# Routing and table writing moved earlier, and the two early-started attentions rearranged, in a twelve-block kernel on one core

## The chip, the cores and the metric

The kernel runs on one core of one Trainium2 chip. The metric is the device time of one execution in microseconds (us). "Before" is the kernel as it stands, "after" the changed one. TensorE does matrix products, VectorE and ScalarE elementwise work, GpSimd elementwise work and the indirect (row by row) transfers, SyncE only issues transfers.

## What is computed

Four layers work in turn on `x` of 4 x 512 x 128 (batch, position, feature), each with a feed-forward part, an attention or recurrence, and the feed-forward part once more. Cut to what matters:

```python
x = x + 0.5 * L0_ffn(layernorm(x))     # moe0_0: 8 experts, best 1, capacity 320
x = x + L0_attn(layernorm(x))          # att0: 16 heads, relative bias, causal
x = x + 0.5 * L0_ffn(layernorm(x))     # moe0_1
x = x + 0.5 * L1_ffn(layernorm(x))     # ffn1_0 (best 2 of 8 gated experts, dense)
x = x + L1_attn(layernorm(x))          # att1
x = x + 0.5 * L1_ffn(layernorm(x))     # ffn1_1
x = x + 0.5 * L2_ffn(layernorm(x))     # ffn2_0 (best 2 of 8 linear experts, dense)
x = x + L2_rec(layernorm(x))           # rec2
x = x + 0.5 * L2_ffn(layernorm(x))     # ffn2_1
x = x + 0.5 * L3_ffn(layernorm(x))     # moe3_0: 8 experts, best 2, capacity 512
x = x + L3_attn(layernorm(x))          # att3: a layernorm, gamma and beta of its own inside, all positions seen
x = x + 0.5 * L3_ffn(layernorm(x))     # moe3_1
```

In a mixture (`moe...`) each token goes to the expert with the highest gate logit (layer 3: to the best two), takes the next free slot of it, in token order, and is dropped when the slots are full. Layer 3 gives slots to all first choices ahead of all second ones.

## The kernel before

`x` stays on the chip as 16 tiles of 128 tokens; a batch `b` (0 to 3) is four tiles. One block of code follows another. A block has a program for each engine, run in order, with semaphores between them, and all engines meet at its end. At some ends the semaphores used so far are cleared as well.

**Routing** (`Routing`). For a batch, `choose` (VectorE) finds the expert from the gate logits, `count` (TensorE) counts earlier tokens of the same expert, `place` (VectorE) makes slot numbers, and `scatter` (GpSimd, L573) issues one indirect transfer for each tile into `dispatched`, a table in HBM. For layer 3 there are `choose(1)`, `count_second`, `place_second` and a second scatter of `second_rows`. The table is first filled with a row that marks a slot as unused (`write_untaken`, L229); no scatter may start before that has landed.

**Mixture** (`moe_capacity`). The load of the first slots waits for all scatters. Eight experts follow (L726, L733). Results go back by indirect transfers (L923) to `returned`, come back as `moe_back`, and VectorE adds them to `x` by batch: `add_rows` (L890), then statistics (`stats`), the power of -1/2 on GpSimd (L108, or L143 for the double norm of layer 3), then the normalised rows (L117 or L150). TensorE transposes these (L172) and ScalarE copies the columns (L184, L181).

**The first block** (`Lead`, in moe0_0) also loads `x` and routes all batches itself. **The start of an attention** (`AttentionStart`, `begun` or `follow`) lies in the mixture ahead of att0 and att3: queries and keys of batch 0 are projected (L1714), taken (L1721) and split into three bf16 parts. High and middle parts are casts on ScalarE; `remainders` (L1734) and `low` (L1740) are subtractions on GpSimd. SyncE writes the parts to HBM (L1751), and loads them back in the form that the score products need (L1759).

**Attention.** Slots `n` from -7 on; slot `n` works on the rows pass of group `n + 2` (L1962: scores, from which VectorE takes maxima, L2343), the columns pass of group `n` (L2002: scores again, with the maximum subtracted, exponentials L2224) and the context of group `n - 1`. Between these, each unit `x` of a slot carries one `turn` with other work: at `n = -4` turn 4 the value projection of batch 0 (L2106, taken by VectorE at turn 5, L2392), which stands alone, since rows passes begin at `n = -2`; at `n = -2` turn 4 a query projection (L2101) of batch 1. Both use `misc_bank`, one bank of PSUM, so the second waits until the first was read. The rows pass has two pairs of banks in turn.

**ffn2_1** (`ffn2`) also routes batches 0 to 2 for moe3_0; moe3_0 routes batch 3.

## Time and profile before

| what | value |
|---|---|
| three runs | 1600.9, 1610.25, 1612.11 us; median 1610.25 |
| profiled execution | 1613.4 us, span 1611.7 us |
| mean granted TensorE clock | 0.866 of full |
| busy: TensorE, VectorE, ScalarE, GpSimd | 1264.2, 836.4, 624.3, 489.3 us |

The span runs from the first to the last instruction. Busy shares are averages over twelve blocks with different limits. The stretches around the block ends, where most engines wait, are what this study reads: the timeline gives, for each group of instructions, start, duration, engine, line, output and inputs, count, and in brackets how long the engine sat idle before it and who ended that.

### The profile page before, as it was taken

The page shows a single profiled execution, that of the slowest core. Times are in us where ns is not written, and L with a number is a line of the kernel's source. Part 1 is how long each engine was busy: PE and PEld are TensorE (multiplying, and loading weights), DVE is VectorE, ACT ScalarE, POOL GpSimd, SP SyncE. Part 2 cuts the span into 40 slices and gives each one's busy share as a digit, 9 for nine tenths or more (in the row PEclk, how much of TensorE's full clock was granted, in tenths as well). Part 3 has the DMA queues.
Part 4 walks back from the last instruction along what each step waited for, and adds up shares of the span by engine and source line. Part 5 has one row for each costly group of instructions (what it writes and reads, how often), then busy time and mean ns, then how long its engine had stood idle before and what let it go on. Part 6 is the DMA issues. An engine that isn't in the chain of part 4 may idle for free. (4 is left out here: it accounts for less than half of the span.)

```text
span 1611.7 us, 25456 instructions
## 1 busy us (share of the span) xinstructions
PE 1264.2 (78%) x9409; PEld 724.5 (45%) x9409; DVE 836.4 (52%) x2167; ACT 624.3 (39%) x1286; POOL 489.3 (30%) x555
## 2 busy tenths in 40 slices
PE   3955899897887956999996977683792799999494
PEld 2543555554564533555553553442561133333273
DVE  4026656551125556667653449675115888883202
ACT  1221444442223223665553214242233377676141
POOL 5552112101330046666400000116473121212443
PEclk9985999896996987999997989686895599998797
DMA  6842422100640007555522700001433312200243
GB/s 129 177 103 70 106 71 68 38 15 11 194 143 10 1 20 216 174 171 150 173 71 38 94 6 2 1 4 43 123 104 88 98 32 70 77 28 15 82 124 112
DMA packets 152549, 131.04 MB, mean 81 GB/s; under 512 B 19393, under 2 KB 138062, under 8 KB 152432
## 3 DMA queue, kind: packets, MB, share of 16 engines
q1 hardware_dynamic: 143136, 116.15, 27.1%
q0 software_dynamic: 6656, 12.00, 2.3%
q10 hardware_dynamic: 2640, 1.36, 0.6%
q8 instruction: 70, 1.15, 0.3%
q14 instruction: 47, 0.39, 0.1%
HBM read 81.86 MB, written 48.37 MB: 81 GB/s over the span
## 5 line engine op out<-in xcount | busy, mean ns | idle before, releaser
L2343 DVE TENSOR_REDUCE att_maxima<-psum 128x2 f32<-128x1024 f32 (+3 forms) x384 | 355.2, 950 | 177.0 <-PE psum L1982 78.0
L2224 ACT ACTIVATE att_probs<-psum 128x512 f32<-128x512 f32 (+1 forms) x640 | 320.7, 554 | 274.8 <-PE psum L2022 114.5
L108 POOL TENSOR_TENSOR rstd<-var_eps,neg_half 128x4 f32<-128x4 f32 x44 | 45.0, 1024 | 560.3 <-DVE var_eps L99 560.3
L923 POOL DMA_INDIRECT returned<-moe_out,moe_slot_tokens x112 | 107.8, 963 | 140.6 <-DVE moe_out L880 107.1
L2002 PE MATMUL psum<-att_queries,att_keys 50*128 50x512 bf16 (+3 forms) x512 | 127.9, 360 | 28.1 <-ACT att_probs L2224 16.9
L172 PE MATMUL psum<-ident,normalised_rows 128*128 128x128 f32 x192 | 44.2, 372 | 125.5 <-DVE normalised_rows L117 86.2
L797 ACT ACTIVATE moe_hidden<-psum,moe_b 128x320 f32<-128x320 f32 (+1 forms) x128 | 77.7, 607 | 130.3 <-PE psum L726 128.7
L733 PE MATMUL psum<-moe_w,moe_hidden 128*128 128x128 f32 (+1 forms) x784 | 111.4, 289 | 0.0
L1962 PE MATMUL psum<-att_keys,att_queries 48*128 48x512 bf16 (+3 forms) x512 | 95.2, 381 | 15.0 <-DVE att_maxima L2343 12.4
L726 PE MATMUL psum<-moe_slot_columns,moe_w 128*128 128x320 f32 (+1 forms) x256 | 99.0, 531 | 2.9 <-ACT moe_slot_columns L792 2.9
L733 PEld LDWEIGHTS psum<-moe_w,moe_hidden 128*128 128x128 f32 (+1 forms) x784 | 92.1, 185 | 15.5 <-issue 8.2
L2061 PE MATMUL psum<-att_probs,att_values 128*32 128x512 f32 (+3 forms) x1024 | 97.8, 458 | 0.8 <-ACT att_context_t L2231 0.8
L573 POOL DMA_INDIRECT dispatched<-normalised_rows,route_scatter_i x64 | 63.7, 995 | 99.3 <-DVE route_scatter_i L553 77.5
L172 PEld LDWEIGHTS psum<-ident,normalised_rows 128*128 128x128 f32 x192 | 30.3, 190 | 139.8 <-DVE normalised_rows L117 84.0
L2046 PE MATMUL psum<-att_probs,att_values 128*32 128x256 f32 x1024 | 86.4, 416 | 1.3 <-ACT att_context_t L2231 1.3
L2002 PEld LDWEIGHTS psum<-att_queries,att_keys 50*128 50x128 bf16 x512 | 37.5, 95 | 96.2 <-ACT att_probs L2224 69.9
L184 ACT COPY normalised_columns<-psum 128x512 f32<-128x512 f32 x44 | 25.8, 586 | 137.2 <-PE psum L172 136.7
L2005 PE MATMUL psum<-att_queries,att_keys 96*128 96x512 bf16 (+3 forms) x256 | 73.4, 303 | 4.5 <-ACT att_probs L2224 4.1
L2022 PE MATMUL psum<-bias_kq,flips 64*128 64x192 f16 (+2 forms) x1024 | 74.5, 256 | 0.0
L1962 PEld LDWEIGHTS psum<-att_keys,att_queries 48*128 48x128 bf16 x512 | 25.9, 96 | 106.5 <-DVE att_maxima L2343 53.3
L2007 PE MATMUL psum<-att_queries,att_keys 98*128 98x512 bf16 (+3 forms) x256 | 69.4, 302 | 0.0
L1247 PE MATMUL psum<-products,normalised_columns 128*128 128x512 f32 x128 | 64.4, 656 | 5.9 <-DVE x_rows L1331 3.8
(266 smaller groups left out, 2200.1 us busy)
## 6 DMA issues: line engine op xcount, KB each, us to landing
score_terms<-att_parts SPq DMA_DIRECT2D x44, 384.0 KB, 2.8
moe_w<-l_w SPq DMA_DIRECT2D x64, 256.0 KB
moe_back<-returned SPq DMA_DIRECT2D x24, 256.0 KB, 4.4
att_queries<-score_terms SPq DMA_DIRECT2D x64, 96.0 KB
att_keys<-score_terms SPq DMA_DIRECT2D x64, 96.0 KB
att_queries<-score_terms SPq DMA_DIRECT2D x16, 384.0 KB, 4.2
att_keys<-score_terms SPq DMA_DIRECT2D x16, 384.0 KB, 5.3
dispatched<-untaken SPq DMA_DIRECT2D x2, 2064.0 KB, 24.6
```

The source lines that it names most:

```text
L172: mm = g.nc.tensor.transpose(bank[:, j * P:(j + 1) * P], g.xn[:, GROUP * b + j, 0:D], g.ident[:])
L726: nc.tensor.matmul(h_bank[c][:, 0:cap], w1_sb[i][:, c * P:(c + 1) * P], dt_sb[i][:], start=True, stop=True).then_inc(h_psum, 1)
L733: mm = nc.tensor.matmul(o_bank[i][0:n, t * D:(t + 1) * D], h_sb[i][:, c, t * P:t * P + n], w2_sb[i][:, c, :], start=(c == 0 and t == 0), s ...
L797: nc.scalar.activation(h_sb[i][:, c, :], h_bank[c][:, 0:cap], ACT.Relu, bias=b1_sb[:, bass.ds(e * CH + c, 1)]).then_inc(h_ready, 1)
L923: nc.gpsimd.indirect_dma_start(out=g.returned[0:choices * TOKENS, :], out_offset=IndirectOffsetOnAxis(ap=slot_token[e % 2][0:m, t:t + 1], ...
L1962: mm = nc.tensor.matmul(dst, q_op[half, i, p, query], k_op[half, i, p, 0:w], start=c0 == 0, stop=kind == 3, skip_group_check=True)
L2002: mm = nc.tensor.matmul(dst, k_op[half, i, p, key], q_op[half, i, p, query], start=c0 == 0, stop=kind == 3, skip_group_check=True)
L2022: mm = nc.tensor.matmul(g.psum[:, cols_bank + r, c0:c0 + seen], flips[half, n, chunk, :], bias_kq[half, pair, chunk, n, 0:seen], start=Fal ...
L2046: mm = nc.tensor.matmul(o_bank[VW * j:VW * (j + 1), 2 * P * half:2 * P * (half + 1)], values[:, G // GROUPS % 2, s, GH * (G % GROUPS) + j, :],
L2061: mm = nc.tensor.matmul(o_bank[VW * j:VW * (j + 1), first_query[s]:T], values[:, b % 2, s, GH * (G % GROUPS) + j, :], probs[:, G % 2, j, o ...
L2224: nc.scalar.activation(probs[:, G % 2, 2 * p + r, unit_at[u]:unit_at[u] + w], g.psum[:, cols_bank + r, 0:w], ACT.Exp).then_inc(probs_ready, 1)
L2343: ins = nc.vector.tensor_reduce(maxima[:, G % 2, t, 2 * p:2 * p + 2], g.psum[:, rows_bank(k):rows_bank(k) + 2, c0:c0 + w], axis=AX, op=ALU ...
```

## The change

1. **Table.** For mixture 0 the "unused" rows are no longer written from one 516-byte row, repeated, from SyncE behind the loads, but from ten rows made side by side (5160 bytes for each partition) in the space of `moe_back`, and ScalarE issues the transfer as its first act. VectorE clears that space first.
2. **Lead.** TensorE runs 12 spare products (`keep_clock`) before the gates have arrived. Per batch it now does transpose, count of the batch before, logits. VectorE places a batch right after choosing it, and makes the rows of batches 2 and 3 between.
3. **Ends of mixtures.** The rows of batch `b - 1` come ahead of the statistics of batch `b`. `remainders` and `low` move from GpSimd to VectorE. The transposes, columns and residual of batch 3 move into the attention's block, ahead of its slots. moe0_0's semaphores are kept for that.
4. **Attention.** The value projection of batch 0 moves from `n = -4` into the first rows slot, `n = -2` (turn 2, taken at turn 3).
5. **ffn2_1 and moe3_0.** First and second choice and `place` of a batch come ahead of the sum of the batch before (`add_shares`); batch 3 is routed there too; GpSimd scatters a batch before the next power. moe3_0 only scatters batch 3.

Core of the diff:

```diff
@@ Lead.sync
-        sp.wait_ge(self.made, 2)
-        write_untaken(g, sp, (0,))
         self.beside.load(sp)
@@ Lead.tensor
+        pe.wait_ge(self.masked, 4)
+        keep_clock(g, pe, g.bank[3], 12)
         pe.wait_ge(self.small_loaded, 16 * 5)
...
+        for b in range(B):
+            ln_transpose(g, pe, ln, b, g.bank[b])
+            if b >= 1:
+                self.routing.count(pe, b - 1, self.rank_bank[b - 1])
+            ln_logits(g, pe, ln, b, g.bank[b])
+        self.routing.count(pe, B - 1, self.rank_bank[B - 1])
@@ Lead.scalar
+        act.wait_ge(self.cleared, 2)
+        act.dma_start(rows.rearrange("(p k j) d -> p k j d", p=P, j=self.clear.shape[1]),
+                      self.clear[:, None, :, :].to_broadcast([P, rows.shape[0] // (P * self.clear.shape[1]), *self.clear.shape[1:]])
+                      ).then_inc(g.untaken_written[0], 16)
@@ Lead.vector
+        nc.vector.memset(self.clear, 0.0).then_inc(self.cleared, 1)
+        v.wait_ge(self.cleared, 1)
+        nc.vector.memset(self.clear[:, :, D:D + 1], OUT_OF_BOUNDS).then_inc(self.cleared, 1)
...
+        for b in range(B):
+            v.wait_ge(ln.logits, b + 1)
+            routing.choose(v, 0, b)
+            if b < 2:
+                ln_rows(g, v, ln, B - 2 + b)
+            routing.place(v, b, self.rank_bank[b])
@@ moe_capacity, vector
+            for b in range(B):
+                add_rows(b, 0)
+                if b == 1 and not last:
+                    rows(0)
+                if choices == 2:
+                    add_rows(b, 1)
+                if last:
+                    continue
+                if follow and b == B - 1 and choices == 1:
+                    follow.remainders(v)
+                if b >= 2:
+                    rows(b - 1)
+                if follow and b == B - 1:
+                    follow.low(v)
+                stats(b)
+                if follow and b == B - 2 and choices == 2:
+                    follow.remainders(v)
+            if not last:
+                rows(B - 1)
@@ ffn2, vector
             for b in range(B):
                 add_pair(b, 0)
+                if 0 <= b - 2 < routed:
+                    route_first(b - 2)
                 if b >= 1:
                     add_shares(b - 1)
-                if 0 <= b - 2 < routed:
-                    route_first(b - 2)
-                    routing.place(v, b - 2, rank_bank)
...
+                route_first(B - 1)
+                routing.place_second(v, B - 1, rank_bank)
@@ AttentionStart
+    def turn_last(self, pe, bank):
+        ln_transpose(self.g, pe, self.ln, B - 1, bank)
+
+    def copy_last(self, act, bank):
+        ln_columns(self.g, act, self.ln, B - 1, bank)
+        if self.twofold:
+            self.twofold.residual(act, B - 1)
@@ attention, tensor
                     if 0 <= n - 2 < NG:
                         turn_context(n - 2)
+                    if n == -2:
+                        project_values(0)
                 elif turn == 4:
-                    if q == 0 and 0 <= b + 1 < B:
+                    if q == 0 and 1 <= b + 1 < B:
                         project_values(b + 1)
...
+            if split:
+                begun.turn_last(pe, g.bank[cols_bank])
             for n, b, q in slots():
                 C, R = 0 <= n < NG, 0 <= n + 2 < NG
+                if n == 0 and split:
+                    pe.wait_ge(begun.ln.xnt, B)
@@ program
-                clear_semaphores(g, ("att0", "route0_1"))
+                clear_semaphores(g, ("att0", "route0_1", "moe0_0"))
...
-            mixture("moe3_0", "l3", first, B - 1, twice=True, prefetch=weights, follow=begun)
+            mixture("moe3_0", "l3", first, B, twice=True, prefetch=weights, follow=begun, scattered=B - 1)
```

VectorE at the end of moe3_0, from the sums of batch 2 on. Before:

```order
987 L890 SCALAR_TENSOR_TENSOR x_rows<-moe_0_back,moe_0_weight,x_rows 128x128 x8
988 L90 BN_STATS stats<-x_rows 128x6 x4
989 L133 BN_AGGR moments<-stats 128x2 x4
990 L135 TENSOR_SCALAR moe_0_ln_var_pair<-moments 128x4
991 L136 TENSOR_SCALAR moe_0_ln_var_pair<-moments 128x4
992 L150 TENSOR_SCALAR normalised_rows<-x_rows,moments,moe_0_ln_rstd_pair 128x128 x4
993 L152 TENSOR_SCALAR moe_0_ln_factor<-moe_0_ln_rstd_pair 128x4
994 L153 SCALAR_TENSOR_TENSOR moe_0_ln_shift<-moments,moe_0_ln_rstd_pair 128x4
995 L890 SCALAR_TENSOR_TENSOR x_rows<-moe_0_back,moe_0_weight,x_rows 128x128 x8
```

The same place now, up to the low parts:

```order
996 L899 SCALAR_TENSOR_TENSOR x_rows<-moe_0_back,moe_0_weight,x_rows 128x128 x8
997 L151 TENSOR_SCALAR normalised_rows<-x_rows,moments,att_ln_rstd_pair 128x128 x4
998 L153 TENSOR_SCALAR att_ln_factor<-att_ln_rstd_pair 128x4
999 L154 SCALAR_TENSOR_TENSOR att_ln_shift<-moments,att_ln_rstd_pair 128x4
1000 L90 BN_STATS stats<-x_rows 128x6 x4
1001 L134 BN_AGGR moments<-stats 128x2 x4
1002 L136 TENSOR_SCALAR att_ln_var_pair<-moments 128x4
1003 L137 TENSOR_SCALAR att_ln_var_pair<-moments 128x4
1004 L1772 TENSOR_TENSOR att_qk<-att_qk,att_parts 128x512 x2
1005 L899 SCALAR_TENSOR_TENSOR x_rows<-moe_0_back,moe_0_weight,x_rows 128x128 x8
1006 L151 TENSOR_SCALAR normalised_rows<-x_rows,moments,att_ln_rstd_pair 128x128 x4
```

The rows (L151) now precede the statistics, and the two remainders (L1772) stand between the statistics of batch 2 and the sums of batch 3, with the low parts behind the rows of batch 2.

TensorE from the last transposes of moe3_0 to att3's first groups (its `normalised_rows` are the rows to be transposed). Before:

```order
2474 L172 MATMUL psum<-ident,normalised_rows 128x128 x12
2475 L593 UNCONDITIONAL_BRANCH
2476 L1942 UNCONDITIONAL_BRANCH
2477 L2106 MATMUL psum<-att_wv,normalised_columns 128x128 x4
2478 L1962 MATMUL psum<-att_keys,att_queries 128x512 x10
2479 L2101 MATMUL psum<-normalised_columns,att_wq 128x512
2480 L1962 MATMUL psum<-att_keys,att_queries 128x512 x16
```

Now:

```order
2477 L173 MATMUL psum<-ident,normalised_rows 128x128 x8
2478 L595 UNCONDITIONAL_BRANCH
2479 L1980 UNCONDITIONAL_BRANCH
2480 L173 MATMUL psum<-ident,normalised_rows 128x128 x4
2481 L2000 MATMUL psum<-att_keys,att_queries 128x512 x6
2482 L2144 MATMUL psum<-att_wv,normalised_columns 128x128 x4
2483 L2000 MATMUL psum<-att_keys,att_queries 128x512 x4
2484 L2139 MATMUL psum<-normalised_columns,att_wq 128x512
2485 L2000 MATMUL psum<-att_keys,att_queries 128x512 x16
```

Four of the twelve transposes crossed the block's end, and the value projection moved behind six of the score products.

GpSimd from ffn2_1 to moe3_0. Before:

```order
206 L108 TENSOR_TENSOR rstd<-var_eps,neg_half 128x4 x2
207 L573 DMA dispatched<-normalised_rows,route_0_scatter_i 4096x129 x4
208 L573 DMA dispatched<-second_rows,route_0_scatter_i 4096x129 x4
209 L108 TENSOR_TENSOR rstd<-var_eps,neg_half 128x4
210 L573 DMA dispatched<-normalised_rows,route_0_scatter_i 4096x129 x4
```

Now:

```order
202 L108 TENSOR_TENSOR rstd<-var_eps,neg_half 128x4
203 L575 DMA dispatched<-normalised_rows,route_0_scatter_i 4096x129 x4
204 L108 TENSOR_TENSOR rstd<-var_eps,neg_half 128x4
205 L575 DMA dispatched<-second_rows,route_0_scatter_i 4096x129 x4
206 L575 DMA dispatched<-normalised_rows,route_0_scatter_i 4096x129 x4
```

The power of a batch now stands between the two scatters of the batch before.

## Rows read from the trace of the kernel before

**Rows 1.** Windows: length, busy PE PEld DVE ACT POOL, PEclk, DMA share, GB/s.

```profile
0.00:8.00 8.00, 0.00 (x0) 0.00 (x0) 5.30 (x40) 1.50 (x2) 4.20 (x14) 1.00 0.66 181
...
1246.00:1270.00 24.00, 15.23 (x46) 4.41 (x48) 19.22 (x21) 1.69 (x3) 5.87 (x7) 0.50 0.33 101
1270.00:1290.00 20.00, 19.12 (x88) 5.24 (x84) 16.46 (x20) 12.60 (x24) 1.17 (x2) 0.55 0.33 108
```

**Rows 2.** Timeline, moe0_0, from the start to the last scatter.

```profile
1.41 0.22 DVE L1591 MEMSET bias_line<- 48x192 uint32 x1
...
5.37 0.66 SPq L229 DMA_DIRECT2D dispatched<-untaken  x1
...
8.17 1.08 PE L172 MATMUL psum<-ident,normalised_rows 128*128 128x128 f32 x4 [8.17 <-DMA gamma_beta<-l_gamma_beta]
...
10.87 1.71 PE L194 MATMUL psum<-gates,normalised_columns 128*128 128x8 f32 x8
...
11.21 2.35 DVE L117 TENSOR_SCALAR normalised_rows<-x_rows,moments,rstd 128x128 f32<-128x128 f32 x8
...
16.80 0.16 DVE L553 SCALAR_TENSOR_TENSOR route_scatter_i<-route_rank,route_expert_from_last 128x4 uint32<-128x4 f32 x1
...
20.56 1.18 POOL L573 DMA_INDIRECT dispatched<-normalised_rows,route_scatter_i  x1 [8.15 <-DVE route_scatter_i L553]
...
39.93 0.97 POOL L573 DMA_INDIRECT dispatched<-normalised_rows,route_scatter_i  x1 [0.30 <-issue]
```

**Rows 3.** Timeline, end of moe0_0 and start of att0.

```profile
131.30 2.26 POOL L1740 TENSOR_TENSOR att_parts<-att_qk,att_parts 128x512 bf16<-128x512 f32 x2
...
132.48 2.69 SPq L1751 DMA_DIRECT2D score_terms<-att_parts  x6
...
138.92 0.72 SPq L1759 DMA_DIRECT2D att_keys<-score_terms  x1
...
141.44 2.05 PE L2106 MATMUL psum<-att_wv,normalised_columns 128*128 128x128 f32 x8 [4.59 <-PEq L53]
...
143.42 0.61 PE L1962 MATMUL psum<-att_keys,att_queries 48*128 48x512 bf16 x2
```

**Rows 4.** Timeline, the last normalised rows of moe0_1.

```profile
491.24 2.35 DVE L117 TENSOR_SCALAR normalised_rows<-x_rows,moments,rstd 128x128 f32<-128x128 f32 x8
```

**Rows 5.** Timeline, end of ffn2_1 and start of moe3_0.

```profile
1078.20 0.19 ACT L203 COPY logits<-psum 128x32 f32<-128x32 f32 x1 [0.88 <-PE psum L194]
...
1083.49 0.16 DVE L553 SCALAR_TENSOR_TENSOR route_scatter_i<-route_rank,route_expert_from_last 128x4 uint32<-128x4 f32 x1
...
1121.44 0.97 POOL L573 DMA_INDIRECT dispatched<-second_rows,route_scatter_i  x1 [0.30 <-issue]
...
1126.77 0.97 POOL L573 DMA_INDIRECT dispatched<-normalised_rows,route_scatter_i  x1 [4.36 <-DVE route_scatter_i L553]
...
1132.64 0.23 DVE L520 TENSOR_TENSOR route_second_products<-psum,route_onehot 128x64 f32<-128x64 f32 x1 [5.41 <-DMA att_keys<-score_terms]
...
1138.47 0.97 POOL L573 DMA_INDIRECT dispatched<-second_rows,route_scatter_i  x1 [0.30 <-issue]
```

**Rows 6.** Timeline, end of moe3_0 and start of att3.

```profile
1222.35 2.31 DVE L890 SCALAR_TENSOR_TENSOR x_rows<-moe_back,moe_weight,x_rows 128x128 f32<-128x128 f32 x8
1222.59 1.67 POOL L143 TENSOR_TENSOR moe_ln_rstd_pair<-moe_ln_var_pair,neg_half 128x8 f32<-128x8 f32 x1 [9.06 <-DVE moe_ln_var_pair L136]
...
1232.30 3.98 DVE L890 SCALAR_TENSOR_TENSOR x_rows<-moe_back,moe_weight,x_rows 128x128 f32<-128x128 f32 x8
...
1238.65 2.69 SPq L1751 DMA_DIRECT2D score_terms<-att_parts  x6
...
1246.66 2.04 PE L2106 MATMUL psum<-att_wv,normalised_columns 128*128 128x128 f32 x8 [3.01 <-PEq L593]
...
1248.81 0.69 DVE L2392 TENSOR_TENSOR att_values<-psum,att_bv 128x512 f32<-128x512 f32 x1 [1.99 <-issue]
...
1256.14 3.49 DVE L2343 TENSOR_REDUCE att_maxima<-psum 128x2 f32<-128x1024 f32 x3 [0.99 <-PE psum L1962]
```

143 lines of the change are left out of this document (68 added, 75 removed).

## Prediction

> **What bounds the kernel now.** I read the windows first, to see which engine fills a stretch, then the timeline around each edit, and there the brackets, which say who ended an idle time. No single engine bounds the whole. At the start it is a transfer: the slot numbers of batch 0 are written at 16.80 to 16.96, but the first scatter starts at 20.56, and its bracket counts 8.15 us of idle GpSimd [rows 2]. The slots were ready 3.6 us before; what came last is the fill of the table, issued at 5.37. From there GpSimd issues sixteen scatters, one each 1.29 us (39.93 less 20.56, over 15 steps), and the experts wait for all of them. At the end of moe0_0 the chain is the parts of queries and keys: the low parts on GpSimd (131.30), SyncE's writes (132.48) and loads (until 139.64), and only then the block ends and TensorE starts at 141.44 [rows 3]. Between ffn2_1 and moe3_0 it is GpSimd's scatters again: the last of ffn2_1 at 1121.44, the next at 1126.77, and after a hole the last at 1138.47 [rows 5]. In att3's first groups VectorE's maxima take turns with TensorE, at a granted clock of 0.50, the lower level of 1.2 GHz; from 1270 TensorE is busy 19.12 of 20 us at 0.55 and is the bound itself [rows 1].
>
> **The start.** Clearing 1290 words costs VectorE at most 1.5 us, by 0.22 us for 192 words [rows 2]; it is busy 5.30 of the first 8 us [rows 1] and waits for `x` after its small writes, so this is hidden. If that cover were gone, 1.5 us would count. The fill is now issued at about 2.4, and not at 5.37. Its price in large pieces is in no row. Bounds: 1.32 MB at the 181 GB/s of the first 8 us is 7.3 us, done near 11; if the 1.05 MB of `x` share that rate, all is done at 1.9 + 2.37 MB / 181 GB/s = 15.0. I take the first, since those 181 GB/s were for pieces of 512 bytes.
> The slots of batch 0: transposes start at 8.17, when the last small load lands, and take 1.1; columns 0.6; logits 1.71 [rows 2] now follow at once, until 11.7; the copy 0.2; five steps of choosing at 0.22 make 13.0; the rows of batch 2, half of 2.35 [rows 2], 14.2; three steps of placing, 14.9. The spare products can take a microsecond off TensorE's part, but VectorE is busy with statistics until 11.3. With an allowance of 0.6 to 0.9 us from a fulfilled wait to the start of an indirect transfer (an estimate), the first scatter starts at 15.5, 5.0 us sooner. Later batches need their slots each 5.2 us and get them each 3 to 4. All sixteen move up, and so do the experts: **-5.0 us**, between -2.5 (fill or `x` late) and -5.6.
>
> **The end of moe0_0 and att0.** In the new order VectorE does, from its first sum at 116.1 to the first low part, four sums of 1.14, three statistics of 1.43, three rows of 1.11 and three subtractions. A subtraction of 128x512 from SBUF on VectorE is in these rows only by its like, 0.69 us [rows 6]. That makes 14.3 us and about 0.3 of waits: 130.7, where the parts were written from 132.48 [rows 3]. SyncE's chain and the block's end come 1.7 us sooner, TensorE's start at 139.7. But TensorE now first turns batch 3 (1.1 us, like the 1.08 of [rows 2]); the loads of the operands end at 137.9 and land some 2.9 us later, so the rows pass starts at 140.85, 2.6 before 143.42 [rows 3]. Then the value projection of 2.05 us [rows 3] lies inside it, and the query projection at turn 4 has to wait until VectorE has read the values, because both use one bank: maxima 1.1 plus 0.69. I lay the six units out at their old lengths and come to the end of the first group at 152.2, as before. So **0 us**; from -1.7 (the values fit in TensorE's gaps) to +0.5. At nothing only because the sooner start pays for it.
>
> **moe0_1.** Its last eight tiles of rows stand in one piece, 2.35 us, with no wait [rows 4]: the rows of batch 2 covered the power of batch 3. Now they come first, and VectorE waits some 1.1 us. TensorE had work left there, so 0.4 to 1.1; I take **+0.4**.
>
> **ffn2_1 and moe3_0.** Choosing ahead of `add_shares` gives the first slots sooner, but VectorE had ended its sums at 1076.45 and the logits are there at 1078.39 [rows 5]: 1.9 us idle, for batch 1 another 1.5. `add_shares` (4.1 us) then follows. The first scatter moves from 1084.5 to about 1082.3, the second batch's by 0.7, but from there VectorE is late by 2 to 3, and it has batch 3 to choose and place too (twice about 1.1, the second count and its placing, 3.5 in all). The block ends with VectorE at 1124.6 instead of with GpSimd at 1122.4 [rows 5], so 2.2 us later. In moe3_0 the eight scatters then run without a hole: before, they began at 1126.77, stood from 1131.6 to 1134.6, and ended at 1139.44, since VectorE came to L520 only at 1132.64 after 5.41 us [rows 5]. Now: start 1125.8, seven steps of 1.29 and the last one's own 0.97 to 1.18, end at 1136.0. With the weights' loads issued 2.2 us later and still in flight, I allow 0.2 for landing: **-3.2 us**, from -4 to -1 (weights last).
>
> **The end of moe3_0 and att3.** Before, GpSimd's remainders lay beside VectorE's sums, and eight sums took 3.98 us, where with the power beside them they took 2.31 [rows 6]. That goes, and four subtractions of 0.7 come. Stepping through the order, the first low part is ready at 1238.7, and the writes had started at 1238.65 [rows 6]: no gain. ScalarE's residual no longer ends the block, worth 0.5, and the turning of batch 3 eats it; the operands land at about 1248.7 as before. Now the first group: VectorE's maxima take 1.16 each (3.49 for three) and the query projection already starves it for 0.99 [rows 6]. The value projection, 2.04 [rows 6], starves it in the same way for 1.0 to 1.2; its taking, 0.69, moves from ahead of the maxima to between them; and the query projection waits for that, 0.5 more. **+2.3 us**, from 0 to +3.5. Nothing swallows it: the next group's maxima follow on the same engine.
>
> A rule bears on the subtractions. The row shows eight sums at 2.31 us although a power of 1.67 us ran beside them [rows 6]. The Trainium skill, SBUF — State Buffer, section "SBUF: two separate sides", says that VectorE with two SBUF inputs and a GpSimd instruction that reads SBUF exclude each other for the whole instruction. By that rule a power would lengthen such work by up to its own 1.6 us, and the sum would be 1.2 us worse; the row does not show it for the power, only for the subtractions.
>
> **The sum.** -5.0 + 0 + 0.4 - 3.2 + 2.3 = -5.5 us, on the profiled execution of 1613.4 us: 1607.9. That execution lies 3.1 us above the median of the three runs, and the term applies to either, so 1610.25 - 5.5 = 1604.7.
>
> **Rivals.**
> (a) The clock comes back sooner in att3. For: it is at the lower level until about 1288, and TensorE, now with 3 us more work in the same stretch of 24 of which it filled 15.23, is the bound from 1270 [rows 1]; full speed from there halves some 18 us: -9, in all 1596. Against: VectorE's starving grows too.
> (b) Slower: the clock comes back later, at both attention starts, because VectorE's first group is longer and TensorE waits in it. Each 10 us more at the lower level in a TensorE-bound stretch costs 5 [rows 1]; at two places 10, in all 1615. It decides from 11 us of added half-speed work on.
> (c) The large pieces crowd out `x` and the small loads, on which TensorE's start hangs (8.17, [rows 2]): the slots come 3.5 us later, 1608.
> (d) VectorE's unexplained standing at L520 is not gone but falls at another place of ffn2_1, where all wait for VectorE: about 4 us, 1609. Against: nothing shows that it must.
> (e) att0 keeps its 1.7 us and att3 loses only 1: 1602.
> (f) The rule above with its whole price, the powers and subtractions shutting each other out: 1606.
>
> **How the numbers follow.** Forecast 0.46, (a) 0.12, (b) 0.12, (c) 0.13, (d) 0.10, (e) 0.10, (f) 0.03, and 0.04 for none of them (an edit that doesn't do what it says: the powers later than the rows need them). The three runs of one kernel lie 11 us apart, so each case is some 4 us wide. From 1597 to 1613 the range leaves out most of (a) and about half of (b). About 1% (16 us) is what a measurement of this kernel can tell from no change. Faster by that needs (a) and the best end of the start: 0.08. Slower by that needs (b) twice over: 0.03. Within: 0.89.
>
> **What would show it.** First scatter of moe0_0 near 15.5, last near 34.9. Low parts of att0 near 130.7, but its first columns pass not over 1 us sooner relative to the experts' end. In moe0_1 an idle of about 1.1 ahead of the last four rows. In ffn2_1 waits of VectorE for logits (1.9, 1.5) and a later block end; in moe3_0 eight scatters without a hole. In att3 two starved stretches of VectorE in the first group in place of one. The prediction is wrong if the granted clock of 1270 to 1290 differs from 0.55 by much, if the fill lands after 15, or if the scatters of ffn2_1 end with the weights' loads and not before.

## The result, and the profile after

Over twelve runs each, the changed kernel has a median of 1614.56 us and the kernel before one of 1608.22: ratio 1.0034, interval 1.0017 to 1.005, so some 5.5 us slower, where 5.5 us faster was forecast (1604.7) and 1613 was the end of the range. Its profiled execution took 1616.63 us, span 1614.9, clock 0.859.

I read the windows of the changed kernel first (columns as in [rows 1]).

```profile
0.00:8.00 8.00, 4.83 (x12) 1.58 (x12) 5.92 (x38) 1.50 (x2) 4.22 (x14) 1.00 0.76 264
8.00:42.00 34.00, 14.84 (x94) 11.78 (x95) 13.87 (x73) 3.66 (x10) 17.46 (x19) 0.54 0.31 91
...
1246.00:1270.00 24.00, 12.67 (x41) 4.50 (x42) 15.70 (x20) 3.00 (x6) 3.53 (x4) 0.50 0.32 99
1270.00:1290.00 20.00, 17.66 (x60) 4.64 (x59) 16.62 (x21) 10.29 (x19) 3.53 (x4) 0.50 0.30 99
```

Two things are new. DMA moves 264 GB/s in the first 8 us in place of 181 [rows 1], and from 8 to 42 us the granted clock is 0.54, where the same window of before has this row:

```profile
8.00:42.00 34.00, 15.42 (x98) 12.43 (x99) 13.41 (x71) 3.65 (x10) 18.99 (x21) 1.00 0.61 112
```

The timeline of the changed kernel at the start, beside [rows 2]:

```profile
2.43 0.58 ACTq L285 DMA_DIRECT2D dispatched<-moe_back  x1
...
2.92 4.05 SPq L262 DMA_DIRECT2D gates<-l_gate  x4
...
7.01 0.46 SPq L263 DMA_DIRECT2D gamma_beta<-l_gamma_beta  x1
...
10.85 1.11 PE L173 MATMUL psum<-ident,normalised_rows 128*128 128x128 f32 x4 [3.00 <-DMA gamma_beta<-l_gamma_beta]
...
17.80 0.16 DVE L555 SCALAR_TENSOR_TENSOR route_scatter_i<-route_rank,route_expert_from_last 128x4 uint32<-128x4 f32 x1
...
18.93 1.19 POOL L575 DMA_INDIRECT dispatched<-normalised_rows,route_scatter_i  x1 [4.69 <-DVE route_scatter_i L555]
...
27.56 0.19 ACT L204 COPY logits<-psum 128x32 f32<-128x32 f32 x1 [4.11 <-remote]
...
28.97 0.54 PE L457 MATMUL psum<-route_onehot,onesb 128*128 128x32 bf16 x15
...
36.19 0.19 DVE L549 TENSOR_TENSOR route_rank_products<-psum,route_onehot 128x32 f32<-128x32 f32 x1 [7.33 <-remote]
...
37.65 0.97 POOL L575 DMA_INDIRECT dispatched<-normalised_rows,route_scatter_i  x1 [3.49 <-DVE route_scatter_i L555]
...
41.48 0.97 POOL L575 DMA_INDIRECT dispatched<-normalised_rows,route_scatter_i  x1 [0.30 <-issue]
```

The same two loads in the timeline of before:

```profile
2.92 1.93 SPq L261 DMA_DIRECT2D gates<-l_gate  x4
...
4.89 0.43 SPq L262 DMA_DIRECT2D gamma_beta<-l_gamma_beta  x1
```

The fill goes out at 2.43. SyncE then takes 4.05 us to issue the four gate loads, where it took 1.93, so `gamma_beta` goes out only at 7.01 (4.89 before) and TensorE's first transposes, which wait for it, start at 10.85 (8.17 before). The slots of batch 0 are there at 17.96, later than the 16.96 of before. The first scatter is still 1.6 us sooner, since the table is ready. Then batch 3, where TensorE answers late twice. Its logits show their end at 25.47, but ScalarE takes them at 27.56. Its count, fifteen small products, stands at 28.97 for 0.54 us, but VectorE, which waits for nothing else, goes on only at 36.19. GpSimd runs dry for 3.49 us, and the last scatter is 1.55 us later than before instead of 5.0 sooner.

The landings (last column, median us from issue), of the changed kernel and then of before:

```profile
dispatched<-moe_back ACTq DMA_DIRECT2D x1, 1290.0 KB, 6.9
x_rows<-x SPq DMA_DIRECT2D x4, 256.0 KB, 7.4
...
gates<-l_gate SPq DMA_DIRECT2D x4, 4.0 KB, 6.1
```

```profile
dispatched<-untaken SPq DMA_DIRECT2D x1, 1290.0 KB, 14.3
x_rows<-x SPq DMA_DIRECT2D x4, 256.0 KB, 4.6
...
gates<-l_gate SPq DMA_DIRECT2D x4, 4.0 KB, 2.9
```

The fill takes 6.9 us in place of 14.3 (7.3 was estimated), and `x` and the gates pay 2.8 and 3.2 us. Pieces, queue and time of issue changed together, so these rows don't show which of them shortened the fill. In the kernels below that issue the same pieces at 6.8 to 8.2 it takes 7.9 to 9.9 us.

Timeline of the changed kernel in ffn2_1 and moe3_0, beside [rows 5]:

```profile
1074.85 0.19 DVE L381 TENSOR_REDUCE route_best<-logits 128x4 f32<-128x32 f32 x1 [1.89 <-ACT logits L204]
...
1091.75 0.19 DVE L381 TENSOR_REDUCE route_best<-logits 128x4 f32<-128x32 f32 x1 [3.27 <-issue]
...
1119.00 0.55 PE L457 MATMUL psum<-route_onehot,onesb 128*128 128x32 bf16 x15
...
1123.40 0.19 DVE L549 TENSOR_TENSOR route_rank_products<-psum,route_onehot 128x32 f32<-128x32 f32 x1 [3.13 <-remote]
...
1128.42 0.97 POOL L575 DMA_INDIRECT dispatched<-normalised_rows,route_scatter_i  x1 [6.58 <-POOLq L53]
...
1137.38 0.97 POOL L575 DMA_INDIRECT dispatched<-second_rows,route_scatter_i  x1 [0.30 <-issue]
...
1141.79 4.52 SPq L662 DMA_DIRECT2D moe_slots<-dispatched  x3
...
1146.02 0.59 ACT L799 COPY moe_slot_columns<-psum 128x512 f32<-128x512 f32 x1 [16.01 <-PE psum L726]
```

VectorE waits for logits 1.89 and 3.27 us, for batch 3's 1.84 us, and 3.13 us for batch 3's count, whose products show their end at 1119.55. I measure this stretch from the first of ffn2_1's second 64 scaled outputs, 1059.58 before and 1056.09 after: block's end at +63.8 before, +71.6 after; last scatter at +78.9 and +81.3; the experts' first slot columns at +84.8 and +89.9. The eight scatters of moe3_0 run without a hole, as forecast, but they start at +72.3, where the forecast had +66.2. From the last scatter to the slot columns it is 8.6 us, against 5.9. So 5.1 us are lost here, where 3.2 were to be won.

Timeline of the changed kernel in att3, beside [rows 6]:

```profile
1241.27 2.69 SPq L1789 DMA_DIRECT2D score_terms<-att_parts  x6
...
1251.41 1.04 PE L2000 MATMUL psum<-att_keys,att_queries 48*128 48x512 bf16 x4 [1.07 <-DMA att_keys<-score_terms]
...
1256.61 1.22 DVE L2389 TENSOR_REDUCE att_maxima<-psum 128x2 f32<-128x1024 f32 x1 [0.99 <-PE psum L2000]
...
1258.49 2.08 PE L2139 MATMUL psum<-normalised_columns,att_wq 128*128 128x512 f32 x2 [1.49 <-DVE att_values L2438]
...
1260.60 0.69 ACT L2287 ACTIVATE att_qk<-psum,att_bq_scaled 128x512 f32<-128x512 f32 x1 [7.91 <-PE psum L2139]
...
1261.15 1.22 DVE L2389 TENSOR_REDUCE att_maxima<-psum 128x2 f32<-128x1024 f32 x1 [1.58 <-PE psum L2000]
```

Two starved stretches of VectorE and TensorE's wait of 1.49 for the values' bank, as described. From the start of att3's block to ScalarE's taking of batch 1's queries it is 11.30 us (1249.30 to 1260.60) against 8.89 before (1246.71 to 1255.60).

### The profile page after: what moved, and what is told of

The parts are those of the page before. It is cut to its first block and busy times, and to the rows that moved or that the text cites. A ratio compares the mean times of both kernels' runs of the same rounds, so it can differ in the third digit from the quotient of the medians.

```text
span 1614.9 us, 25496 instructions
## 1 busy us (share of the span) xinstructions
PE 1268.1 (79%) x9421; PEld 723.5 (45%) x9421; DVE 836.7 (52%) x2177; ACT 624.6 (39%) x1286; POOL 482.2 (30%) x547
```

## The experiments

The five sets ran on chips of two levels: before had medians of 1614, 1609 and 1609 us in three sets (1608 in the first comparison), and of 1578 in two. Ratios stand against the runs of before on the same chip; I call the two levels the slower and the quicker chip. The changed kernel was compared on the slower. joined and fill_behind_x rest on six runs each, late_fill on eleven, the others on twelve.

| kernel | chip | ratio | 95% interval |
|---|---|---|---|
| start_only | quicker | 0.9997 | 0.9983 to 1.0011 |
| route_only | quicker | 1.0027 | 1.0009 to 1.0046 |
| ends_only | quicker | 1.0001 | 0.9982 to 1.002 |
| no_spare | quicker | 1.0018 | 1.0003 to 1.0033 |
| changed_again | slower | 1.0025 | 0.9999 to 1.005 |
| late_fill | slower | 0.9939 | 0.9913 to 0.9964 |
| route_weights_first | slower | 0.9983 | 0.9957 to 1.0008 |
| ends_values_back | slower | 0.996 | 0.9934 to 0.9985 |
| late_fill_no_spare | slower | 0.996 | 0.9937 to 0.9983 |
| weights_first | slower | 0.999 | 0.9964 to 1.0017 |
| joined | slower | 0.9917 | 0.9887 to 0.9948 |
| joined_routed | slower | 0.9962 | 0.994 to 0.9985 |
| order_alone | quicker | 1.0003 | 0.9982 to 1.0024 |
| batch3_alone | quicker | 1.0009 | 0.9982 to 1.0036 |
| joined_again | quicker | 0.9959 | 0.9937 to 0.9981 |
| fill_behind_x | quicker | 0.9918 | 0.9892 to 0.9944 |
| fill_x_again | slower | 0.9987 | 0.9961 to 1.0012 |
| fill_x_batch3 | slower | 0.9949 | 0.9929 to 0.9968 |

### The parts one by one

Three kernels have one part of the change each, the fourth is the changed kernel less one line.

```diff
@@ no_spare: Lead.tensor
         pe.wait_ge(self.masked, 4)
-        keep_clock(g, pe, g.bank[3], 12)
         pe.wait_ge(self.small_loaded, 16 * 5)
```

> The kernel before with the edits of the table and of Lead alone (parts 1 and 2 of the change), nothing else. Theory A (the start costs, because the large pieces delay the loads and the spare products disturb TensorE): as in the changed kernel, the last scatter of moe0_0 starts near 41.5 and not at 39.93, the granted clock of 8 to 42 us is near 0.5, and the time is 1 to 2 us above before. Theory B (the late count of batch 3 in the changed kernel, whose wait of 7.33 us stood ahead of the last four scatters, was an accident of that one execution): the last scatter starts near 38 and the time is 1 to 2 us below before.

> The kernel before with the edits of ffn2_1 and moe3_0 alone (part 5). Theory A (the routing of batch 3 in ffn2_1 is paid in full on VectorE and TensorE, and the block's end costs more than the hole that it closes): from the middle of ffn2_1 to the first columns of the experts (before at 1144.39) 3 to 5 us are lost, ratio 1.002 to 1.003. Theory B (my term of -3.2 us holds and the profiled shift is the drift of the clock ahead of it): 1 to 3 us faster, ratio 0.998 to 0.999.

> The kernel before with the edits of the mixtures' ends and of the attention's start alone (parts 3 and 4: rows ahead of statistics, remainders and low parts on VectorE, the turning of batch 3 in the attention's block, the value projection at n = -2). Theory A (att3's start pays): about 2.5 to 3.5 us slower in all, of which att3's first group is 2.4 and the low parts and operands the rest, and att0 between 0 and 0.5. Theory B (what att3's start loses TensorE makes up behind it, since it is the bound from 1270): within 1 us of before.

> The changed kernel without the twelve spare products at the start. Theory A (they take TensorE to the lower granted clock from 10 to 45 us and with it comes the late end of batch 3's count): the granted clock of 8 to 42 us returns to 1.00, the wait of 7.33 us at L549 is gone, the last scatter starts near 38 in place of 41.48, and the time is about 3 us below the changed kernel. Theory B (the count is late for another reason, such as the order of transposes, counts and logits on TensorE): the last scatter stays near 41.5 and the time within 1 us of the changed kernel.

The route part alone makes 0.27%, 4.3 us of 1578, of which the positions below show 2.2. The start and the ends come out even. In start_only the first scatter starts at 18.56 and the last at 37.89; in ends_only, which has the old start, at 20.57 and 39.95. The experts' first columns come at 43.68 and 46.26. So the start is worth 2.1 to 2.6 us on the quicker chip, not 5.0. The ratio doesn't show them, though its interval (-2.7 to +1.7 us) allows them. In ends_only att3's first group is 2.2 us longer (11.11 against 8.89), and the ratio of 1.0001, good to 3 us, neither shows nor excludes that. In start_only theory B was right on the late count. Its row, at the place where the changed kernel stood for 7.33 us:

```profile
26.54 0.54 PE L456 MATMUL psum<-route_onehot,onesb 128*128 128x32 bf16 x15
27.21 0.19 DVE L548 TENSOR_TENSOR route_rank_products<-psum,route_onehot 128x32 f32<-128x32 f32 x1 [0.78 <-PE psum L456]
```

The windows of 8 to 42 us, of start_only and then of no_spare:

```profile
8.00:42.00 34.00, 18.26 (x109) 12.95 (x109) 13.86 (x73) 3.66 (x10) 20.53 (x24) 0.60 0.33 98
```

```profile
8.00:42.00 34.00, 17.81 (x105) 13.01 (x106) 13.88 (x73) 3.66 (x10) 20.12 (x23) 1.00 0.31 94
```

The spare products bring the lower clock: 0.60 with them, 1.00 without, for nearly the same work. But on this chip nothing follows from it: the last scatter of no_spare starts at 38.50.

### The start mended, the weights, the values

```diff
@@ late_fill: the start part alone, and in Lead.scalar, ahead of the fill
+        for b in range(B):
+            act.wait_ge(self.loaded[b], 16)
+        act.wait_ge(self.small_loaded, 16 * 5)
         act.dma_start(rows.rearrange(...
@@ route_weights_first: the route part alone, and in moe_capacity, sync
-            elif prefetch:
-                prefetch.load(sp)
...
             if lead:
                 zero_returned(g, sp, 0)
+            if prefetch:
+                prefetch.load(sp)
@@ ends_values_back: the ends part alone, with project_values(0) and take_values(0) at n = -4
```

> The changed kernel, unedited, on another chip day. Theory A (the two late answers of TensorE, 6.6 us at batch 3's count of moe0_0 and 3.7 us in ffn2_1, belong to the execution and the chip, not to the order): they are absent as they were in the four runs before, the last scatter of moe0_0 starts near 38, and the ratio is about 1.002 to 1.003, which the route part alone gave (1.0027). Theory B (they belong to the changed kernel as a whole, since the partial kernels did not have it together): the wait of several us at L549 is there again and the ratio is 1.003 to 1.005.

> The kernel before with the start's edits alone, as start_only, but ScalarE issues the table's transfer only when x and the small loads have landed. Theory A (the fill took bandwidth from x, gates and gamma, whose landing moved TensorE's first transposes from 8.17 to about 11): the transposes start at 8 to 8.5, the slots of batch 0 are ready near 15, the fill (6.9 us in one piece at 2.43) is done by 15 to 16, the first scatter starts at 15.5 to 16.5 and the last near 35.5, 2 us ahead of start_only, and the time is about 2 to 4 us below before. Theory B (it is the new order on TensorE that is late, or the fill is then last): the first scatter stays at 18 to 19 and the time within 1 us of start_only's (ratio 0.9997).

> The kernel before with the route part alone, as route_only, but in moe3_0 (and nowhere else with effect) SyncE issues the attention's weights behind the experts' weights and the slots, so the first experts' weights go out some 3.8 us sooner. Theory A (in route_only the later block end made the experts' weights and the transfers around the slots last, so that the slots arrived 7.8 us behind the last scatter and the first hidden products ran at 1.7 us apart): slots near 6.5 us behind the last scatter, the first four hidden 0.86 to 1.3 us apart, and 2 to 3 us below route_only, ratio 0.999 to 1.001. Theory B (the first products are slow because the granted clock has fallen, which weights do not change): spacing of 1.3 to 1.7 us stays and the ratio is 1.002 to 1.003.

> The kernel before with the ends' edits, as ends_only, but the value projection of batch 0 stays at n = -4, as before. Theory A (the value projection between the first maxima starves VectorE, my term of +2.3 us): from att3's block start to ScalarE's taking of batch 1's queries 9.0 to 9.5 us in place of 11.3, and 1 to 3 us below ends_only. Theory B (values at n = -4 delay the first scores by 2 us, so that it comes out even): within 1 us of ends_only.

The changed kernel repeats itself on the slower chip, if at 1.0025 and with an interval that just reaches 1. Its timeline at batch 3's count:

```profile
28.31 0.54 PE L457 MATMUL psum<-route_onehot,onesb 128*128 128x32 bf16 x15
...
35.50 0.19 DVE L549 TENSOR_TENSOR route_rank_products<-psum,route_onehot 128x32 f32<-128x32 f32 x1 [7.29 <-remote]
```

So the late answer is no accident of one execution (theory A fell): it came both times that this kernel ran on the slower chip. late_fill, with the fill behind the loads, has transposes at 7.90 and the slots at 14.59, as my working had (8.17 and 14.9):

```profile
7.90 0.63 PE L172 MATMUL psum<-ident,normalised_rows 128*128 128x128 f32 x4 [0.22 <-DMA gamma_beta<-l_gamma_beta]
7.91 0.63 ACTq L289 DMA_DIRECT2D dispatched<-moe_back  x1
...
14.43 0.16 DVE L557 SCALAR_TENSOR_TENSOR route_scatter_i<-route_rank,route_expert_from_last 128x4 uint32<-128x4 f32 x1
...
18.02 1.19 POOL L577 DMA_INDIRECT dispatched<-normalised_rows,route_scatter_i  x1 [5.36 <-DVE route_scatter_i L557]
```

Now the fill is last: the scatter starts only at 18.02, 3.4 us behind its slots. Still the last one starts at 37.36 against 41.96 and 41.83 in the two kernels of this set with the old start, 4.5 us sooner, and the ratio is 0.9939. Theory A, in part: what fell short is the fill's end. Two things temper this. The old start was itself slower in this set (fill landed after 16.3 and 16.2 us against 14.3 in before, first scatters at 22.61 and 22.49 against 20.56), and 0.61% is 9.8 us, of which the start shows about half; where the rest comes from, no row of the start shows.

In route_only the first slot columns come 7.8 us behind the start of the last scatter (+76.7 to +84.5, from the point in ffn2_1 that was named above), in route_weights_first 6.2 (+79.5 to +85.7). The ratios, 1.0027 and 0.9983, are of two chips and carry nothing here. The positions do, when all kernels are laid side by side. Where the first load of moe3_0's experts (`moe_b`) was issued 6.0 to 6.5 us ahead of the last scatter (changed, changed_again, route_only, batch3_alone), the slot columns came 7.5 to 8.6 us behind that scatter. Where it was issued 8 us or more ahead (before, start_only, order_alone and those with the weights behind the slots), they came 5.9 to 6.6 behind it. So the loads delay the slots' when too little time lies between them and the last scatter, and issuing the attention's weights later gives that time back. ends_values_back has 9.64 us (1239.04 to 1248.68) to the taking of batch 1's queries, against 11.11 in ends_only (1223.55 to 1234.66): 1.5 of the 2.2 us by the values, 0.7 by the turning of batch 3 ahead of the scores, if the two chips may be compared in this stretch. Its ratio is 0.996, lower than theory A had it and lower than any position of it explains.

### Joined, and what is left of the route part

```diff
@@ joined: start and ends parts; late_fill, no spare products, values at n = -4, weights behind the slots; routing as before the change
@@ joined_routed: as joined, with the route part
@@ weights_first: the kernel before, with the weights behind the slots alone
```

> The kernel before with the start's edits, the fill issued behind the loads as in late_fill, and without the twelve spare products. Theory A (the spare products bring the lower granted clock from 10 to 40 us, and on a chip with times above 1600 a late answer of TensorE with it): clock of 8 to 42 us at 1.00, no matmul of a count later than 1 us behind its modelled end, first scatter at 15.5 to 16.5 and not 18.02, last near 35.5; 1 to 2 us below late_fill, ratio 0.992 to 0.995. Theory B (the low clock comes from the steady work of the new order, without the spare products as well): first scatter at 18, ratio near 0.994 to 0.996.

> The kernel before with one edit: in moe3_0 SyncE issues the attention's weights behind the experts' weights and the slots. It tells what part of route_weights_first's gain against route_only was the order of the weights and what belonged to the late block end. Theory A (only a late block end makes the weights last): within 1 us of before, ratio 0.9995 to 1.0005. Theory B (the weights are last in before too): slots arrive about 1 us sooner behind the last scatter (before: 5.9 us from 1138.48 to 1144.39), ratio 0.998 to 0.999; then the route part costs nothing by it either and was slower by the same in both.

> Joined: the start's edits with the late fill and without spare products, the ends' edits with the value projection at n = -4, the weights behind the slots in moe3_0, and the routing of ffn2_1 and moe3_0 as before the change. If the parts add (late fill 0.994, ends with values back 0.996, weights 0.999 to 1), 0.988 to 0.991 of before; if what one gains at a block's end is taken back by the granted clock behind it, 0.993 to 0.996.

> As joined, but with the route part of the change (batch 3 routed in ffn2_1). Theory A (the route part costs 3 to 4 us whatever the order of the weights, by the block's end that VectorE sets 2 to 3 us later): 2 to 4 us above joined. Theory B (with the experts' weights ahead, what is left of it is a gain, since route_weights_first came out at 0.9983): 0 to 3 us below joined.

joined is at 0.9917, a little short of the parts added, joined_routed at 0.9962 on the same chip. That is 0.45%, some 7 us, for the route part (theory A, and more than it said), but the two intervals overlap. From the point in ffn2_1 the slot columns come at +84.2 and +87.2, so 3.0 us are seen in the traces. Without the spare products the clock of late_fill_no_spare is 1.00 again from 8 to 42 us, but the count is 1.4 us late, where it was 1.05 in late_fill, and the first scatter starts at 19.11 behind a fill of 9.9 us, the last at 38.46. Neither theory held. weights_first brings the slots from 5.9 to 6.1 us behind the last scatter, no gain, and 0.999 cannot be told from 1.

The route part has two halves. I took them apart on the quicker chip.

```diff
@@ order_alone: ffn2, vector and gpsimd; batch 3 is routed in moe3_0
                 add_pair(b, 0)
+                if 0 <= b - 2 < routed:
+                    route_first(b - 2)
                 if b >= 1:
                     add_shares(b - 1)
@@ batch3_alone: ffn2, vector; moe3_0 only scatters batch 3, all else in the old order
                 routing.place_second(v, B - 2, rank_bank)
+                route_first(B - 1)
+                routing.place(v, B - 1, rank_bank)
+                routing.place_second(v, B - 1, rank_bank)
@@ fill_behind_x: joined, less one line in Lead.scalar
-        act.wait_ge(self.small_loaded, 16 * 5)
```

> The kernel before with one half of the route part: in ffn2_1 the choices and the placing of a batch come ahead of the sum of the batch before, and GpSimd scatters first choices ahead of the next power; batch 3 is routed in moe3_0 as before. Theory A (the cost is the late block end by batch 3): within 1.5 us of before, 0.999 to 1.001, the block's end at 152 to 153 us behind ffn2_1's first scaled output is not later than in before (there 1123.29 less 1059.58, 63.7 us behind the first of the second half). Theory B (the reorder makes VectorE wait for logits, 1.9 and 3.3 us in the changed kernel, and delays the sums): 2 to 4 us slower, 1.0015 to 1.0025.

> The kernel before with the other half: batch 3 is chosen, counted and placed at the end of ffn2_1, and moe3_0 only scatters it; the order of all else as before. Theory A (this is the cost): the block's end 2.5 to 3.5 us later, the experts' weights issued as much later, first slot columns about 2 us later, ratio 1.0015 to 1.003. Theory B: the hole between the two groups of scatters in moe3_0 closes (GpSimd stood 3 us at L572 before) and the time is 1 to 3 us below before.

> The kernel joined, unedited, a second time, since 6 fast runs stood behind it: 0.990 to 0.994 of before if the 0.9917 holds.

> joined, but the fill waits only for x and not for the five small loads. Theory A (the first scatter waits for the fill: slots of batch 0 ready at 14.4 to 15.3, scatter at 17.7 to 19.1): the fill goes out about 1.5 us sooner (6 to 6.5 in place of 7.91), the first scatter starts near 16.5, and the time is 0.5 to 1.5 us below joined_again. Theory B (gates and gamma are crowded out again, transposes at 9 to 10): first scatter at 17.5 to 18, no difference within 1 us.

Measured from the same point as above (the first of ffn2_1's second 64 scaled outputs), quicker chip:

| kernel | block's end | last scatter | first slot columns |
|---|---|---|---|
| start_only (old routing) | +63.7 | +76.0 | +82.3 |
| order_alone | +66.5 | +78.8 | +84.7 |
| batch3_alone | +63.7 | +73.8 | +81.3 |
| route_only (both) | +66.6 | +76.7 | +84.5 |

The order is what costs: 2.8 us at the block's end, and these rows of order_alone say why.

```profile
1057.18 0.19 DVE L379 TENSOR_REDUCE route_best<-logits 128x4 f32<-128x32 f32 x1 [1.89 <-ACT logits L203]
...
1074.07 0.19 DVE L379 TENSOR_REDUCE route_best<-logits 128x4 f32<-128x32 f32 x1 [3.26 <-ACT logits L203]
```

VectorE stands for 5.15 us ahead of sums that it could have done meanwhile. The old order has no wait over 0.7 us there until the last batch. Batch 3's routing costs nothing at the block's end on this chip and brings the last scatter 2.2 us forward, of which 1.0 reaches the slots; the rest goes to the loads, which were issued only 6.5 us ahead of it. As times, order_alone (1.0003) and batch3_alone (1.0009) cannot be told from before, nor from half of route_only's excess each; the positions, not the ratios, carry this.

fill_behind_x issues the fill at 6.77 with the transposes still at 7.85; slots at 14.92, first scatter at 15.89, last at 35.26:

```profile
6.77 0.58 ACTq L288 DMA_DIRECT2D dispatched<-moe_back  x1
...
7.85 1.09 PE L173 MATMUL psum<-ident,normalised_rows 128*128 128x128 f32 x4 [7.85 <-DVE normalised_rows L117]
...
15.89 1.18 POOL L576 DMA_INDIRECT dispatched<-normalised_rows,route_scatter_i  x1 [3.29 <-DVE route_scatter_i L556]
```

These are nearly the 15.5 and 34.9 of my prediction, reached by another edit than the one it was made for. The experts' first columns come at 41.22, against 46.37 in order_alone and 46.91 in batch3_alone with the old start on the same chip: 5.2 and 5.7 us sooner, where 5.0 were forecast.

> The kernel fill_behind_x, unedited, a second time: 0.990 to 0.994 of before on either kind of chip, if the 0.9918 of 6 runs holds; first scatter near 16 and last near 35.5.

> As fill_behind_x, with batch 3 chosen, counted and placed at the end of ffn2_1 and only scattered in moe3_0 (the edits of batch3_alone, the old order of all else). Theory A (with the experts' weights ahead of the attention's, the sooner scatters reach the experts): first slot columns 80 to 81.5 us behind the block's first share in place of 82.2, and 1 to 2 us below fill_x_again. Theory B (the landing of the scatters' data is last, and the spare products end too soon before the slots): columns at 82 or later and no difference within 1 us; on a chip with times above 1600 TensorE's late answer to batch 3's count may then push the block's end and cost 2 to 4 us.

On the slower chip the first scatter is at 15.92 again, but batch 3's count is late (VectorE goes on at 33.32, 5.3 us behind the end of the products), and the last scatter starts at 38.61:

```profile
27.45 0.54 PE L458 MATMUL psum<-route_onehot,onesb 128*128 128x32 bf16 x15
33.32 0.19 DVE L550 TENSOR_TENSOR route_rank_products<-psum,route_onehot 128x32 f32<-128x32 f32 x1 [5.98 <-remote]
```

The ratio of 0.9987 can't be told from 1, so the 0.9918 did not hold on this chip. fill_x_batch3, with batch 3's routing in ffn2_1, is at 0.9949; its interval overlaps that of fill_x_again, and its slot columns come at +83.0 against +83.6. As theory B said, a late answer to batch 3's count (VectorE waits 4.61 us in ffn2_1) pushes the block's end, yet the time is not worse for it. Both ratios near 0.992 were of six runs, and both came back nearer to 1 with twelve runs on the other kind of chip. joined (0.9917, 0.9959) beat the kernel before on both chips; fill_x_batch3 was tried on one.

## Why the prediction was wrong

**The start: -5.0 forecast, +1.9 in the profile (experts' first columns at 47.43 against 45.58).** Clearing was hidden, the fill took 6.9 us as estimated, and choosing and placing took the time that I gave them. The step that failed is the one that let TensorE begin at 8.17, as before: it began at 10.85. I had written the other end ("fill or `x` late", -2.5) and rival (c), 3.5 us, and gave it 0.13. Transposes at 10.85 and slots at 17.96 are rival (c), nearly to its number. late_fill and fill_behind_x show the cause by taking it away: transposes at 7.9, slots at 14.6 and 14.9. I asked what sharing does to the fill (done near 11 or at 15.0) and put its effect on the small loads at nothing in the sum. Of the 2.7 us, 2.1 lie ahead of `gamma_beta`'s issue (SyncE took 4.05 us over the four gate loads in place of 1.93) and 0.6 in its landing (3.8 us for 3.2); the gate loads themselves took 6.1 us to land in place of 2.9. The spare products are not the cause: no_spare has none and its transposes start at 11.06. The Trainium skill, DMA: Bandwidth & Descriptors, section "Queues, rings and completion order", says that each DMA engine goes round between the queue rows that have work, a packet at a time, and that SyncE's and ScalarE's transfers have a row each. The landings agree with that rule. What late_fill and fill_behind_x show is that the loads are late while the fill is in flight beside them; no run moved the queue or the piece size alone, so neither is shown to matter by itself. On the quicker chip the term was -2.1 by the last scatter and -2.6 by the experts' first columns, about my bound of -2.5.

The late slots cost 3.4 us against the forecast (first scatter at 18.93 for 15.5). The other 3.2 us are no step of mine: the answer to batch 3's count comes 6.7 us behind its products, and GpSimd stands for 3.49 us. Rival (d) had named such a standing, "at another place of ffn2_1"; it fell in ffn2_1 and at the start.

**ffn2_1 and moe3_0: -3.2 forecast, +5.1 in the profile, +2.2 on the quicker chip.** Three terms failed. First, the hole: I read VectorE's 5.41 us at L520 [rows 5] as part of the order, to be closed by routing batch 3 sooner. It holds a late answer of TensorE, whose last product there ends 3.5 us ahead of VectorE's step, and only the slower chip has that. In start_only VectorE comes to the same instruction after 1.53 us, and the last scatter starts at +76.0 in the old order too, not at +78.9:

```profile
1106.27 0.23 DVE L521 TENSOR_TENSOR route_second_products<-psum,route_onehot 128x64 f32<-128x64 f32 x1 [1.53 <-PE psum L474]
```

On the quicker chip 2.2 us were there to win (batch3_alone). On the slower the hole closed and the late answer fell in ffn2_1 instead, as rival (d) had it: 3.13 us of waiting for batch 3's count, ahead of the block's end. Second, the waits for logits: I had 1.9 and 1.5, they are 1.9 and 3.3, and every later sum of the block waits with them. The block's end, forecast 2.2 us later, was 2.8 later on the quicker chip and 7.8 on the slower. Third, the landing: I allowed 0.2 us for loads still in flight. It was 1.5 in route_only (last scatter to slot columns 7.8 us, against 6.3 in start_only) and 2.7 in the changed kernel (8.6 against 5.9). My own bound for this case, "weights last", was only -1.

**att0: 0 forecast.** Right in each step. From the first sum to the first write of parts it is 14.48 us (117.97 to 132.45) against 16.42 before, 1.9 sooner (1.7 forecast); the first scores start 2.9 sooner relative to that sum's shift (2.6 forecast); and ScalarE's taking of batch 1's queries, +1.56 where the first sum was at +1.9, shows that all but 0.35 was given back.

**moe0_1: +0.4 forecast.** The wait is there to the figure, 1.12 us, and from the sums of batch 1 to the next block's start it is 19.42 us (482.43 to 501.85) against 19.14, so +0.3:

```profile
494.68 1.11 DVE L117 TENSOR_SCALAR normalised_rows<-x_rows,moments,rstd 128x128 f32<-128x128 f32 x4 [1.12 <-POOL rstd L108]
```

**att3: +2.3 forecast.** 2.4 measured in the first group, in the way described; ends_only and ends_values_back part 2.2 of it into 1.5 and 0.7. The end of moe3_0, forecast at nothing, cost another 1.0 (first slot columns to att3's start 103.3 us, against 102.3).

The profiled pair adds up as +1.9 (start), +5.1 (ffn2_1, moe3_0), +1.0 and +2.4 (att3), 10.4 in all, of which 3.2 are left at the end. 5.3 were regained between moe0_0's experts and ffn2_1, 3.2 of them behind att1's start, in blocks that the change does not touch, and 1.9 behind att3's first group. The stretch of the 5.3 us is 1014.0 us in before and 1008.7 after, and 992 and 1001 in order_alone and route_only, which are alike there: it is the spread of single executions. The parts, not that sum, carry the finding. Rivals (a) and (b) were about when the clock comes back in att3. In windows of 1 us it is back 44.7 us behind the block's start in the changed kernel (1294) and 41.3 behind it before (1288); over all kernels with the old start of att3 it is 40 to 46. So (a) did not come, and (b), which needed 11 us, did not either; the 0.50 for 0.55 of 1270 to 1290 only says that the return now lies behind 1290. The chances in my list add up to 1.10 and not to 1, so each of them is too high by about a tenth. Rival (f): eight sums beside a power took 2.38 us here, 2.31 in [rows 6], so the power hardly locks VectorE out. The eight sums that took 3.98 us beside GpSimd's subtractions take 2.37 us with the subtractions gone, as the prediction had it:

```profile
1230.97 2.38 DVE L899 SCALAR_TENSOR_TENSOR x_rows<-moe_back,moe_weight,x_rows 128x128 f32<-128x128 f32 x8
1231.21 1.64 POOL L144 TENSOR_TENSOR att_ln_rstd_pair<-att_ln_var_pair,neg_half 128x8 f32<-128x8 f32 x1 [4.09 <-DVE att_ln_var_pair L137]
```

## What to carry to other kernels

A bulk transfer that is made sooner can be paid by the small loads that something waits for: here it was, and issuing it behind `x` cured it. Look at when the small ones are issued and land, not only at its own rate. When an engine is to do the urgent thing first, ask whether its input is there: work placed behind a wait of 3.3 us is not sooner but later, on the engine that ends the block. And a wait in a trace that no instruction explains is not a hole that an edit closes; find out first whether it is there in another execution, on another chip. Last, a ratio of six runs that looks best of many is likely to shrink: repeat it before you rest on it.

## What the runs showed of the hardware

**Late answers of TensorE.** The fifteen small products of a count (128x32, bf16) show 0.54 us in the trace, yet the engine that waits for them goes on later than that. For batch 3's count of moe0_0, from the products' end to VectorE's next step:

| chip, order of transposes, counts, logits | kernel: gap in us |
|---|---|
| slower, new | changed 6.7, changed_again 6.6, fill_x_again 5.3, fill_x_batch3 5.3, joined 3.1, joined_routed 2.9, late_fill_no_spare 1.4, late_fill 1.05 |
| slower, old | before 0.3, weights_first 0.5, route_weights_first 0.13, ends_values_back 0.13 |
| quicker, new | start_only, no_spare, joined_again, fill_behind_x: 0.13 to 0.14 |
| quicker, old | route_only, ends_only, order_alone, batch3_alone: 0.13 to 0.14 |

So at the start it takes the new order and the slower chip together. The logits of batch 3, just ahead, are late too in four of these kernels: by 2.1 us in the changed kernel both times, by 3.6 and 3.5 in fill_x_again and fill_x_batch3. Logits and count together make 8.7 to 8.9 us in all four. In moe3_0 the old order has it too, at the step of L520: 3.5 us in before, late_fill and late_fill_no_spare, 2.0 to 2.9 in others of the slower chip, none on the quicker. Where batch 3 is counted in ffn2_1 it falls there: 3.9 us in the changed kernel both times, 5.3 in joined_routed and fill_x_batch3, 2.2 in route_weights_first; on the quicker chip it is 0.1 to 0.7. The granted clock doesn't decide it: 0.54 and 0.56 in the changed kernel, but fill_x_again has no stretch at the lower level before 71 us. What does is open; no row shows where TensorE's time goes between these records, and no run was made for that.

**Spare products at the start.** Twelve of them, 128x512, kept TensorE busy from 3.0 to about 8 us. In the changed kernel it then stood for 3.00 us until the transposes. In the four kernels that have them and the new order (changed, changed_again, start_only, late_fill) the granted clock fell to the lower level between 10 and 13 us and stayed there until 39 to 45, a mean of 0.54 to 0.60 over 8 to 42; without them it was 1.00 there. The logits of batch 0 took 1.88 us both at the lower level (12.64, changed kernel) and at full speed (12.83, no_spare), so the level cost these products nothing that the rows show.
